# A two-layer Mamba and attention kernel: the scan's B and C rows in one PSUM bank, the freed bank for projections, outputs and turned rows

## The chip, the cores and the metric

One core of one Trainium2 chip runs the whole program in one launch. The metric is the device time of a launch in microseconds (us). A core has five engines that each work through their own queue in order: TensorE (PE), VectorE (DVE), ScalarE (ACT), GpSimd (POOL) and SyncE (SP, which here only starts DMAs). They wait for each other by semaphores. PE writes into PSUM, 8 banks of 128 partitions x 512 float32; DVE and ACT read it.

## The reference

The input is 8 sequences of 512 tokens with 128 features. Two residual layers follow each other.

```
x = x + mamba_and_filter(layernorm(x)) + mixture_of_2_experts(layernorm(x))     # layer 0
x = x + attention(layernorm(x)) + routed_experts(layernorm(x))                  # layer 1

# the scan of layer 0, for each of 256 inner features and 16 states n:
h[t] = exp(delta[t] * A[n]) * h[t-1] + delta[t] * B[t, n] * u[t]
y[t] += h[t] * C[t, n]

# the attention of layer 1, 16 heads of 64, causal, q and k rotated (rope):
attn = softmax(q k^T / 8);  out = (attn v) wo^T + bo

# routed experts: each token goes to its best 2 of 8 experts, silu(x W1) * (x W3) W2
```

## The kernel before

The 8 sequences are pipelined. Each pass of the loop ("lap") has two phases for sequence b. Phase 1 runs the rest of layer 0 for b (`filter_step`), the routed experts of b-1 (`token_use`), the start of layer 0 for f = b+1 (`front_start`) and that sequence's first two scan states (`early_scan`). Phase 2 runs the attention of b together with the other 14 scan states of f, gathers the expert rows of b-1 and scatters the token rows of b. Every engine's order is written out by hand in its own `phase_1` and `phase_2`. Lap 0 has no b-1, lap 7 no f.

The attention has 8 pairs of heads. A pair takes 4 steps (t_ = 0 to 3, one per 128 query tokens), so phase 2 has 32 steps s. A step handles two score tiles, n = 2s and 2s+1 (one per head), of width (t_+1) x 128. For a tile the work goes around three engines: PE makes the scores (`scores`, L1006 and L1009), DVE takes the row maximum (`largest`, L1803), ACT the exponential (`exponentials`, L1304), PE transposes the result (`turn`, L1017), ACT copies it out of PSUM (`copy_turned`, L1312), PE multiplies with the values (`weigh_values`, L1032). Scores of step s+2 are made in step s. At t_ = 0 DVE divides the pair before by its sums (`divide`, L1815).

The queries and keys of the pair after next are projected in steps t_ = 2 and 3 (`project`, L994). Projection m passes DVE (`rotate`, L1797, which multiplies by the sine into ROT3), SP (`swap_pairs`, a DMA from ROT3), ACT (`add_bias`, L1288) and POOL (`add_rotated`, L1936 and L1939). In steps t_ = 1 PE transposes the finished output of the pair before (`turn_out`, L1041) and ACT copies it (`copy_out`, L1322). Step 12 transposes the gathered rows (`give_back`, L929), steps 24, 26, 27 and 28 the routed rows (`turn_rows`, L890).

A scan state n has three parts on DVE (`front_step`): part 0 (D, L1504) multiplies DU with B row n, part 1 (the scan, L1509) needs exponentials from ACT (DA, L1191), part 2 (H, L1531) multiplies with C row n into HC, which POOL adds to Y (L1925). B and C rows are spread over the partitions by a matmul each (`front_b`, L767, into bank FB; `front_c`, L774, into bank FC). The table `PIECES` says in which step each part stands.

Banks in phase 2: FB and FC for the scan, G2 for turned tiles, G3 for attention sums, and a ring of four (G1, G0, FM, G4) for scores. Projections, outputs and turned rows have no bank of their own: the table `loan` lends them ring bank `RING[2*s % 4]` between score tile 2s and score tile 2s+4. A borrower therefore waits until the exponential of tile 2s has been read (`(p_exp, 2*s_+1)`), and score tile 2s+4 waits until the borrower has been read. PE issues the projection of step s already in step s-1, before `weigh_values`. DVE's `rotate` stands first in step s, ahead of `largest`; ACT's `add_bias` or `copy_out` stands second in step s, behind the first `copy_turned`.

DVE has one more wait in phase 2: `number_places` in step 9 (L1784) waits until POOL has added the gathered rows of b-1 (`add_picks`, L1955, at tile 17).

Of the kernel before, what the change touches and what calls it, by code (L numbers as in the profile page):

```python
# [35 lines left out]
P = 128  # L36
# [87 lines left out]
def build(nc, xT, weights, vecs, conv_rows, dt_w, a_log, moe, experts,  # L124
          row_biases, cos, sin, identity, causal, row_of, in_u_w, outT):
    ctx = ExitStack()
    with ctx:
# [348 lines left out]
        loan = {}  # L476
        for s_ in range(STEPS):
            j_, t_ = s_ // TILES, s_ % TILES
            if s_ < 2:
                loan[s_] = (("proj", 2 + s_), (biased, 3 + s_))  # L480
            if t_ in PROJECT_AT and j_ + 2 < PAIRS:
                m_ = 2 * (j_ + 2) + PROJECT_AT.index(t_)
                loan[s_] = (("proj", m_), (biased, m_ + 1))
            if t_ == OUT_STEP and j_:
                loan[s_] = (("out", j_ - 1), (ot_copy, j_))
            if s_ == RETURN_STEP:
                loan[s_] = (("return", 0), (out_d, 0))
            if s_ in TURN_STEPS and s_ not in loan:
                g_ = TURN_STEPS.index(s_)
                loan[s_] = (("turn", g_), (xt_copy, g_ + 1))  # L490
# [10 lines left out]
        ring_bank["out", PAIRS - 1], ring_free["out", PAIRS - 1] = RING[0], [(p_exp, N_TILES - 3)]  # L501
        assert len(set(k for k, _ in loan.values())) == len(loan)
# [164 lines left out]
        def _(pe):  # L667
# [88 lines left out]
            def front_b(b, n, filtered=None, bank=FB):  # L756
# [8 lines left out]
                if filtered is not None and n == EARLY:  # L765
                    pe.wait_ge(xn2_d.sem, xn2_d.at(filtered))
                pe.matmul(bank[:, :], pick[:, n, :], S3[:, :], start=True, stop=True).then_inc(b_mm.sem, 1)  # L767

            def front_c(b, n, filtered=None):
# [4 lines left out]
                pe.matmul(FC[:, :], pick[:, STATES + n, :], S3[:, :], start=True, stop=True).then_inc(c_mm.sem, 1)  # L774

# [294 lines left out]
            def phase_2(b, f, t):  # L1070
# [4 lines left out]
                if f is not None:  # L1075
                    front_b(f, EARLY, b)
                    front_c(f, EARLY, b)
                values_in(b, f)
                rows_out(b)
                rank(b)  # L1080
# [6 lines left out]
                project(b, 2)  # L1087
                for s in range(STEPS):
                    j, t_ = s // TILES, s % TILES
                    key = loan[s][0] if s in loan else (None, None)  # L1090
                    following = loan[s + 1][0] if s + 1 in loan else (None, None)
                    if key[0] == "out":
# [7 lines left out]
                    turn(b, 2 * s)  # L1100
                    if s:
                        weigh_values(b, 2 * s - 1)
                    if f is not None:
                        for n, part in PIECES[s]:
                            if part == 0:
                                front_b(f, n, b)
                            elif part == 1:
                                front_c(f, n, b)
                    turn(b, 2 * s + 1)
# [32 lines left out]
        def _(act):  # L1142
# [190 lines left out]
            def phase_2(b, f, t):  # L1333
# [10 lines left out]
                for s in range(STEPS):  # L1344
                    copy_turned(b, 2 * s)
                    key = loan[s][0] if s in loan else (None, None)
                    if key[0] == "proj":
                        add_bias(b, key[1])
                    elif key[0] == "out":
                        copy_out(b, key[1])  # L1350
                    elif key[0] == "turn":
                        rows_turned(b, key[1])
# [11 lines left out]
                    if s + 1 < STEPS:  # L1364
                        exponentials(b, 2 * s + 3, f)
                copy_out(b, PAIRS - 1)
# [11 lines left out]
        def _(dve):  # L1378
# [119 lines left out]
            def front_step(b, n, part, early=False):  # L1498
# [602 lines left out]
```

## Time and profile before

| | |
|---|---|
| three runs | 2735.15 us median, 2718.67 to 2745.57 |
| the profiled execution | 2738.27 us, of which the span 2736.5 |
| PE busy | 2185.6 us, 80% of the span |
| DVE busy | 1644.7 us, 60% |
| ACT busy | 1177.2 us, 43% |
| POOL busy | 936.8 us, 34% |
| mean granted PE clock | 0.869 of full |
| chain that ended last | PE 49%, issue 17%, DVE 15%, POOL 9%, ACT 7% |

Busy is the time in which an engine has an instruction of its own in work. The granted clock is the share of 2.4 GHz that PE was given; it has two levels, 1.2 and 2.4 GHz, so 0.50 in a stretch is the lower one throughout. A wait is named by who waited and whose instruction released it.

### The profile page before, as it was taken

How to read it: one execution, taken by the hardware profiler on the slowest of the kernel's cores; microseconds unless marked ns; L12 is line 12 of the kernel's file. 1: busy time of each engine (PE TensorE's matmuls, PEld its weight loads, DVE VectorE, ACT ScalarE, POOL GpSimd, SP SyncE). 2: the span in 40 equal slices, each digit the busy share in tenths (PEclk: the TensorE clock that was granted, in tenths of full speed). 3: DMA queues.
4: the chain of work that ended last, by engine and by line, in shares of the span. 5: the costliest groups of instructions: out<-in, count | busy, mean ns of one | idle time of the engine just before them, and what ended most of it. 6: DMA issues, size and time to landing. Idle time of an engine off the chain costs nothing.

```text
span 2736.5 us, 38788 instructions
## 1 busy us (share of the span) xinstructions
PE 2185.6 (80%) x11640; PEld 1519.0 (56%) x11640; DVE 1644.7 (60%) x2929; ACT 1177.2 (43%) x2702; POOL 936.8 (34%) x581
## 2 busy tenths in 40 slices
PE   4257888888888788888889788987889788888885
PEld 1033566655665556655566556655666555665664
DVE  2965775557754776547764587546765477644322
ACT  2223454345533455345543465333553345423541
POOL 0421562028410473006620185103740067202501
PEclk8568889888999889989899898898899988999997
DMA  2000011311222111321113112221113211131123
GB/s 94 0 16 0 32 50 62 113 51 46 68 82 75 53 41 58 106 76 41 51 64 104 61 46 70 70 88 50 44 59 97 85 37 56 59 126 58 62 93 115
DMA packets 82452, 175.06 MB, mean 64 GB/s; under 512 B 11448, under 2 KB 42560, under 8 KB 81984
## 3 DMA queue, kind: packets, MB, share of 16 engines
q1 hardware_dynamic: 78144, 164.05, 17.9%
q0 software_dynamic: 4096, 8.40, 1.1%
q8 instruction: 107, 1.75, 0.3%
q14 instruction: 105, 0.86, 0.1%
HBM read 123.71 MB, written 15.14 MB: 51 GB/s over the span
## 4 chain that ended last, share of the span: by engine, by line
PE 49%; issue 17%; DVE 15%; POOL 9%; ACT 7%; DMA 1%; SPq 0%; DVEq 0%; POOLq 0%; ACTq 0%
PE G L910 8%; PE G L1032 6%; DVE HS L1509 3%; PE G L1017 3%; POOL Y L1925 3%; PE G L921 2%; PE FM L1006 2%; POOL REG L1936 2%; PE G L1049 2%; PE FM L731 2%; POOL YG L1950 2%; DVE maxes L1803 2%; PE G L1006 2%; POOL REG L1939 2%; PE FM L880 2%
## 5 line engine op out<-in xcount | busy, mean ns | idle before, releaser
L1032 PEld LDWEIGHTS G<-REG 128*128 128x128 f32 x2560 | 376.8, 213 | 79.2 <-issue 53.6
L1032 PE MATMUL G<-REG 128*128 128x64 f32 x2560 | 383.7, 286 | 18.9 <-DVE REG L1815 18.9
L1312 ACT ACTIVATE REG<-G 128x128 f32<-128x128 f32 (+3 forms) x512 | 224.1, 438 | 374.9 <-PE G L1017 371.5
L1509 DVE TENSOR_TENSOR_SCAN HS<-DA,D 128x1024 f32<-128x1024 f32 x128 | 361.8, 2827 | 31.3 <-ACT DA L1191 30.7
L1925 POOL TENSOR_TENSOR Y<-Y,HC 128x1024 f32<-128x1024 f32 x114 | 274.8, 2410 | 258.0 <-DVE HC L1531 257.4
L910 PEld LDWEIGHTS G<-XGT,MW 128*128 128x128 f32 x1920 | 294.9, 238 | 58.1 <-issue 58.1
L910 PE MATMUL G<-XGT,MW 128*128 128x128 f32 x1920 | 301.9, 324 | 19.5 <-DMA MW<-moe 19.5
L1936 POOL TENSOR_TENSOR REG<-REG,cos_t 128x512 f32<-128x512 f32 x128 | 170.4, 1331 | 341.8 <-ACT REG L1288 340.7
L1017 PE MATMUL G<-ident,REG 128*128 128x128 f32 x1280 | 248.1, 295 | 31.0 <-ACT REG L1312 29.4
L1006 PE MATMUL G<-REG 64*128 64x128 f32 (+3 forms) x768 | 233.4, 517 | 12.1 <-ACT REG L1288 6.1
L1261 ACT ACTIVATE SL<-G 128x512 f32<-128x512 f32 x120 | 71.6, 597 | 375.9 <-PE G L910 375.9
L1676 DVE SCALAR_TENSOR_TENSOR SL<-SL,G 128x512 f32<-128x512 f32 x120 | 82.5, 688 | 237.1 <-ACT SL L1261 237.1
L1939 POOL TENSOR_TENSOR REG<-REG 128x512 f32<-128x512 f32 x128 | 200.6, 1567 | 48.5 <-DMA REG<-ROT 36.8
L1191 ACT ACTIVATE DA<-DELTA,a_neg 128x511 f32<-128x511 f32 x256 | 180.8, 721 | 63.2 <-DVE HS L1509 62.9
L1304 ACT ACTIVATE REG<-G,maxes 128x128 f32<-128x128 f32 (+3 forms) x384 | 196.9, 513 | 18.1 <-DVE maxes L1803 18.1
L1017 PEld LDWEIGHTS G<-ident,REG 128*128 128x128 f32 x1280 | 158.7, 154 | 78.1 <-issue 70.8
L1803 DVE TENSOR_REDUCE maxes<-G 128x1 f32<-128x128 f32 (+3 forms) x384 | 165.7, 459 | 27.1 <-PE G L1009 27.0
L1504 DVE TENSOR_TENSOR D<-DU,FB 128x1024 f32<-128x1024 f32 x114 | 138.4, 1214 | 40.4 <-PE FB L767 37.8
L1903 POOL TENSOR_SCALAR Y<-US,V_ 128x512 f32<-128x512 f32 x16 | 24.8, 1559 | 387.7 <-ACT US L1165 353.8
L1909 POOL TENSOR_TENSOR DU<-DELTA,US 128x1024 f32<-128x1024 f32 x8 | 18.8, 2350 | 388.6 <-DVE DELTA L1496 388.6
L921 PE MATMUL G<-MW,HC 128*128 128x128 f32 x960 | 142.7, 297 | 9.9 <-DVE HC L1683 9.9
L921 PEld LDWEIGHTS G<-MW,HC 128*128 128x128 f32 x960 | 133.8, 215 | 11.5 <-DVE HC L1683 8.0
(284 smaller groups left out, 3972.0 us busy)
## 6 DMA issues: line engine op xcount, KB each, us to landing
MW<-moe SPq DMA_DIRECT2D x120, 768.0 KB, 4.3
REG<-ROT SPq DMA_DIRECT2D x256, 128.0 KB
EW<-experts SPq DMA_DIRECT2D x16, 514.5 KB, 4.2
XG<-x_rows SPq DMA_DIRECT2D x8, 960.0 KB, 5.6
y_rows<-YO SPq DMA_DIRECT2D x120, 64.0 KB, 1.5
X<-xT SPq DMA_DIRECT2D x8, 256.0 KB, 5.7
W<-weights SPq DMA_DIRECT2D x1, 2048.0 KB, 9.4
REG<-xT SPq DMA_DIRECT2D x8, 256.0 KB, 2.8
```

What stands on the lines that cost most here:

```text
L910: mm = pe.matmul(G[g + half][:, c * P:(c + 1) * P], MW[:, i % SLOTS, at:at + P], XGT[:, i, :], start=True, stop=True)
L921: mm = pe.matmul(G[4][:, 0:D], HH[:, i % 4, c * P:(c + 1) * P], MW[:, i % SLOTS, 2 * HID + c * D:2 * HID + (c + 1) * D], start=c == 0, sto ...
L1006: pe.matmul(bank[:, 0:width], QK[lo:lo + DK, j % 2, 0, t * P:(t + 1) * P], QK[lo:lo + DK, j % 2, 1, 0:width], start=True, stop=False)
L1017: mm = pe.transpose(G[2][:, c * P:(c + 1) * P], PR[:, n % 2, c * P:(c + 1) * P], ident[:, :])
L1032: mm = pe.matmul(G[3][:, col:col + DK], PT[:, n % 2, c * P:(c + 1) * P], V[:, c, j * P + h * DK:j * P + (h + 1) * DK], start=c == 0, stop= ...
L1304: act.activation(PR[:, n % 2, 0:width], ring_bank[("score", n)][:, 0:width], ACT.Exp, bias=maxes[:, j % 2, at:at + 1], accum_out=rows[:, j ...
L1312: act.activation(PT[:, n % 2, 0:width], G[2][:, 0:width], ACT.Copy).then_inc(pt_copy.sem, 1)
L1509: dve.tensor_tensor_scan(HS[:, :, :].rearrange("p h s -> p (h s)"), DA[:, n % 2, :, :].rearrange("p h s -> p (h s)"), D1[:, :, :].rearrang ...
L1803: dve.tensor_reduce(maxes[:, j % 2, at:at + 1], ring_bank[("score", n)][:, 0:width], AX.X, ALU.max, negate=True).then_inc(nm_d.sem, 1)
L1925: pool.tensor_tensor(Y[:, :, :], Y[:, :, :], HC_EARLY if early else HC[:, n % 2, :, :], ALU.add).then_inc(y_add.sem, 1)
L1936: pool.tensor_tensor(rotated, rotated, cos_t[:, :], ALU.mult).then_inc(rope_d.sem, 1)
L1939: pool.tensor_tensor(rotated, rotated, REG[:, 8 + m % 2, :], ALU.add).then_inc(rope_d.sem, 1)
```

## The change

The scan's B and C rows of states 2 to 15 take turns in FB. A new `main_b` waits until H of the state before has read its C row, a new `main_c` until D of its own state has read the B row. FC becomes `MISC`, the bank of all projections, outputs and turned rows of phase 2 (`guest` in place of `loan`); each guest waits for the guest before it to be read, and scores wait for exponentials only. The guest's PE work moves behind `turn(b, 2*s+1)` of its own step s, `rotate` and `give_back` move to the end of DVE's step, `add_bias`, `copy_out` and `rows_turned` to the end of ACT's step. Part 2 of a state is placed by an offset of 1.45 in place of 1.7, which brings H of states 4, 6, 8 and 15 one step forward. The front loop of lap 0 and the early scan keep their banks.

```diff
@@ tables
-                PIECES[int(at_ + (0.0, 0.7, 1.7)[part_])].append((n_, part_))
+                PIECES[int(at_ + (0.0, 0.7, 1.45)[part_])].append((n_, part_))
+        PICKS_AT = {s_: [] for s_ in range(STEPS)}
+        for n_ in range(FIRST, STATES):
+            d_ = next(s_ for s_ in PIECES if (n_, 0) in PIECES[s_])
+            h_ = next(s_ for s_ in PIECES if (n_, 2) in PIECES[s_])
+            PICKS_AT[d_].append((n_, 0))
+            PICKS_AT[max(d_ + 1, h_ - 1)].append((n_, 1))
...
-            if n_ >= 4 and n_ % 2 == 0 and n_ // 2 - 2 in loan:
-                ring_free["score", n_] = [loan[n_ // 2 - 2][1]]
-        for s_, (key, freed) in loan.items():
-            ring_bank[key], ring_free[key] = RING[2 * s_ % 4], [(p_exp, 2 * s_ + 1)]
+        freed_ = []
+        for s_, (key, freed) in guest.items():
+            ring_bank[key], ring_free[key], freed_ = MISC, freed_, [freed]
@@ PE
+            def main_b(b, n, filtered):
+                if n == EARLY:
+                    pe.wait_ge(xn2_d.sem, xn2_d.at(filtered))
+                pe.wait_ge(hc_mul.sem, hc_mul.at(b, n))
+                pe.matmul(FB[:, :], pick[:, n, :], S3[:, :], start=True, stop=True).then_inc(b_mm.sem, 1)
+            def main_c(b, n):
+                pe.wait_ge(db_mul.sem, db_mul.at(b, n + 1))
+                pe.matmul(FB[:, :], pick[:, STATES + n, :], S3[:, :], start=True, stop=True).then_inc(c_mm.sem, 1)
@@ PE, phase_2
-                project(b, 2)
                 for s in range(STEPS):
...
+                    turn(b, 2 * s)
+                    if s:
+                        weigh_values(b, 2 * s - 1)
+                    if f is not None:
+                        for n, part in PICKS_AT[s]:
...
+                    turn(b, 2 * s + 1)
+                    if key[0] == "proj":
+                        project(b, key[1])
+                    elif key[0] == "out":
                         turn_out(b, key[1])
...
-                    if following[0] == "proj":
-                        project(b, following[1])
@@ ACT, phase_2
                     copy_turned(b, 2 * s)
-                    if key[0] == "proj":
-                        add_bias(b, key[1])
...
                         exponentials(b, 2 * s + 3, f)
+                    if key[0] == "proj":
+                        add_bias(b, key[1])
@@ DVE, phase_2
-                    if key[0] == "proj":
-                        rotate(b, key[1])
                     if s + 1 < STEPS:
                         largest(b, 2 * s + 2)
                         largest(b, 2 * s + 3)
...
                         for n, part in PIECES[s]:
                             front_step(f, n, part)
+                    if key[0] == "proj":
+                        rotate(b, key[1])
```

The instruction order shows three places. In it `HS<-DA,D` is the scan, `ROT<-` is `rotate`, `maxes<-` is `largest`, and `HC<-` and `D<-` are H and D of a state.

DVE before, lap 0, from H of state 2 (ahead of step 0) to the start of step 1:

```order
L1531 TENSOR_TENSOR HC<-HS,FC 128x1024
L1797 SCALAR_TENSOR_TENSOR ROT<-G,V_,sin_t 128x512
L1803 TENSOR_REDUCE maxes<-FM 128x1
L1803 TENSOR_REDUCE maxes<-G 128x1
L1504 TENSOR_TENSOR D<-DU,FB 128x1024
L1509 SCALAR_TENSOR_TENSOR HS<-DA,D 128x1024
L1797 SCALAR_TENSOR_TENSOR ROT<-FM,V_,sin_t 128x512
```

DVE after, the same place:

```order
L1549 TENSOR_TENSOR HC<-HS,FB 128x1024
L1821 TENSOR_REDUCE maxes<-FM 128x1
L1821 TENSOR_REDUCE maxes<-G 128x1
L1522 TENSOR_TENSOR D<-DU,FB 128x1024
L1527 SCALAR_TENSOR_TENSOR HS<-DA,D 128x1024
L1815 SCALAR_TENSOR_TENSOR ROT<-FC,V_,sin_t 128x512
```

The first `rotate` (projection 2) moved from ahead of D and the scan of state 3 to behind them, and reads FC.

ACT before, lap 0, steps 0 and 1 (L1312 `copy_turned`, L1288 `add_bias`, L1304 exponentials, L1191 DA):

```order
L1312 ACTIVATE REG<-G 128x128
L1288 ACTIVATE REG<-G,V_ 128x512
L1304 ACTIVATE REG,rows<-FM,maxes 128x256
L1191 ACTIVATE DA<-DELTA,a_neg 128x511
L1312 ACTIVATE REG<-G 128x128
L1191 ACTIVATE DA<-DELTA,a_neg 128x511
L1304 ACTIVATE REG,rows<-G,maxes 128x256
L1312 ACTIVATE REG<-G 128x256
```

ACT after, the same place (L1330 `copy_turned`, L1306 `add_bias`, L1322 exponentials, L1209 DA):

```order
L1330 ACTIVATE REG<-G 128x128
L1322 ACTIVATE REG,rows<-FM,maxes 128x256
L1209 ACTIVATE DA<-DELTA,a_neg 128x511
L1330 ACTIVATE REG<-G 128x128
L1209 ACTIVATE DA<-DELTA,a_neg 128x511
L1322 ACTIVATE REG,rows<-G,maxes 128x256
L1306 ACTIVATE REG<-FC,V_ 128x512
L1330 ACTIVATE REG<-G 128x256
```

`add_bias` moved from behind the first copy of its step to directly ahead of the first copy of the next step.

PE before, lap 0, steps 0 and 1 (L994 projection, L1017 `turn`, L767 and L774 B and C row, L1006 and L1009 scores, L1032 `weigh_values`):

```order
L994 MATMUL G<-XN,W 128x512
L1017 MATMUL G<-ident,REG 128x128
L767 MATMUL FB<-S,pick 128x512
L774 MATMUL FC<-S,pick 128x512
L1017 MATMUL G<-ident,REG 128x128
L1006 MATMUL G<-REG 128x384 x2
L1009 MATMUL G<-causal_bf,ident_bf 128x128 x2
L994 MATMUL FM<-XN,W 128x512
L1032 MATMUL G<-REG 128x64
L1017 MATMUL G<-ident,REG 128x128 x2
```

PE after, the same place (L1010 projection, L1033 `turn`, L786 and L790 B and C row, L1022 and L1025 scores, L1048 `weigh_values`):

```order
L1033 MATMUL G<-ident,REG 128x128
L786 MATMUL FB<-S,pick 128x512
L1033 MATMUL G<-ident,REG 128x128
L1010 MATMUL FC<-XN,W 128x512
L1022 MATMUL G<-REG 128x384 x2
L1025 MATMUL G<-causal_bf,ident_bf 128x128 x2
L1048 MATMUL G<-REG 128x64
L1033 MATMUL G<-ident,REG 128x128 x2
L1048 MATMUL G<-REG 128x64
L790 MATMUL FB<-S,pick 128x512
```

Both projections stand one turn later, and the C row of state 3 moved from beside its B row into step 1.

## Rows read from the trace of the kernel before

**Rows 1.** The page: shares of the chain that ended last, by engine.

```profile
PE 49%; issue 17%; DVE 15%; POOL 9%; ACT 7%; DMA 1%; SPq 0%; DVEq 0%; POOLq 0%; ACTq 0%
```

**Rows 2.** Windows, phase 2 of laps 2 and 7: stretch, length, busy by engine, PEclk, DMA.

```profile
924.00:1094.00 170.00, 144.84 (x833) 98.82 (x831) 121.45 (x172) 96.51 (x259) 107.85 (x66) 0.89 0.15 51
...
2504.00:2634.00 130.00, 112.86 (x772) 80.44 (x771) 54.41 (x128) 79.20 (x228) 58.38 (x50) 1.00 0.18 61
```

**Rows 3.** Waits over the whole span: total us, times, longest us.

```profile
PE FM L994 <- ACT REG L1304: 54.9, 48, 4.2
PE G L994 <- ACT REG L1304: 54.7, 48, 2.7
...
PE G L1017 <- ACT REG L1312: 29.4, 116, 0.5
...
DVE place_i L1784 <- POOL YG L1955: 24.9, 7, 5.1
```

**Rows 4.** Windows inside phase 2 of lap 2.

```profile
936.00:985.00 49.00, 38.73 (x238) 24.88 (x234) 38.07 (x55) 30.04 (x84) 43.53 (x27) 0.96 0.13 44
985.00:1005.00 20.00, 17.80 (x74) 13.51 (x75) 12.26 (x19) 7.57 (x21) 16.05 (x11) 0.50 0.16 57
1005.00:1032.00 27.00, 20.50 (x129) 13.22 (x128) 23.53 (x23) 16.61 (x45) 15.90 (x10) 1.00 0.23 74
1032.00:1046.00 14.00, 14.00 (x65) 11.04 (x64) 6.69 (x11) 5.22 (x16) 6.12 (x4) 0.51 0.06 20
```

**Rows 5.** Timelines of DVE, ACT, PE around 1028 us: start, us, engine, line, idle before.

```profile
1025.50 3.46 DVE L1509 TENSOR_TENSOR_SCAN HS<-DA,D 128x1024 f32<-128x1024 f32 x1 [1.11 <-ACT DA L1191]
1028.89 0.72 DVE L1797 SCALAR_TENSOR_TENSOR ROT<-G,V_,sin_t 128x512 f32<-128x512 f32 x1
...
1029.64 0.69 ACT L1288 ACTIVATE REG<-G,V_ 128x512 f32<-128x512 f32 x1 [1.96 <-DVE ROT L1797]
1030.24 0.69 ACT L1304 ACTIVATE REG<-FM,maxes 128x512 f32<-128x512 f32 x1
...
1031.07 1.13 PE L994 MATMUL FM<-XN,W 128*128 128x512 f32 x2 [2.72 <-ACT REG L1304]
```

**Rows 6.** Timelines of POOL, DVE, PE around 984 us.

```profile
982.39 1.26 POOL L1955 TENSOR_TENSOR YG<-YG 128x512 f32<-128x512 f32 x1
...
983.85 0.17 DVE L1784 CAST place_i<-places 128x8 uint32<-128x8 f32 x1 [5.12 <-POOL YG L1955]
...
985.25 0.61 PE L774 MATMUL FC<-S,pick 96*128 96x512 bf16 x1 [2.72 <-DVE HC L1531]
...
988.45 2.08 PE L994 MATMUL FM<-XN,W 128*128 128x512 f32 x2 [1.95 <-ACT REG L1304]
```

**Rows 7.** Timelines of DVE, ACT, POOL in steps 0 and 1 of lap 2.

```profile
937.80 0.75 DVE L1797 SCALAR_TENSOR_TENSOR ROT<-G,V_,sin_t 128x512 f32<-128x512 f32 x1 [0.46 <-PE G L994]
...
941.15 2.29 DVE L1509 TENSOR_TENSOR_SCAN HS<-DA,D 128x1024 f32<-128x1024 f32 x1 [0.80 <-ACT DA L1191]
...
938.59 0.69 ACT L1288 ACTIVATE REG<-G,V_ 128x512 f32<-128x512 f32 x1 [0.40 <-DVE ROT L1797]
...
941.81 0.38 ACT L1312 ACTIVATE REG<-G 128x256 f32<-128x256 f32 x1 [0.23 <-PE G L1017]
...
939.73 1.27 POOL L1936 TENSOR_TENSOR REG<-REG,cos_t 128x512 f32<-128x512 f32 x1
...
945.72 1.28 POOL L1936 TENSOR_TENSOR REG<-REG,cos_t 128x512 f32<-128x512 f32 x1
```

**Rows 8.** PE timeline: eight value matmuls at the full and at the half clock.

```profile
1037.34 1.81 PE L1032 MATMUL G<-REG 128*128 128x64 f32 x8
...
1071.28 1.00 PE L1032 MATMUL G<-REG 128*128 128x64 f32 x8
```

**Rows 9.** Waits in lap 7's phase 2.

```profile
PE G L994 <- ACT REG L1304: 4.4, 7, 0.8
PE FM L994 <- ACT REG L1304: 3.9, 6, 0.7
```

More of the change, by code:

```diff
@@ L479, in build @@
             if s_ < 2:
-                loan[s_] = (("proj", 2 + s_), (biased, 3 + s_))
+                guest[s_] = (("proj", 2 + s_), (biased, 3 + s_))
             if t_ in PROJECT_AT and j_ + 2 < PAIRS:
                 m_ = 2 * (j_ + 2) + PROJECT_AT.index(t_)
-                loan[s_] = (("proj", m_), (biased, m_ + 1))
+                guest[s_] = (("proj", m_), (biased, m_ + 1))
             if t_ == OUT_STEP and j_:
-                loan[s_] = (("out", j_ - 1), (ot_copy, j_))
+                guest[s_] = (("out", j_ - 1), (ot_copy, j_))
             if s_ == RETURN_STEP:
-                loan[s_] = (("return", 0), (out_d, 0))
-            if s_ in TURN_STEPS and s_ not in loan:
+                guest[s_] = (("return", 0), (out_d, 0))
+            if s_ in TURN_STEPS and s_ not in guest:
                 g_ = TURN_STEPS.index(s_)
-                loan[s_] = (("turn", g_), (xt_copy, g_ + 1))
+                guest[s_] = (("turn", g_), (xt_copy, g_ + 1))
         ring_bank, ring_free = {}, {}
@@ L1086, in phase_2 @@
                 scores(b, 1)
-                project(b, 2)
                 for s in range(STEPS):
                     j, t_ = s // TILES, s % TILES
-                    key = loan[s][0] if s in loan else (None, None)
-                    following = loan[s + 1][0] if s + 1 in loan else (None, None)
-                    if key[0] == "out":
+                    key = guest[s][0] if s in guest else (None, None)
+                    turn(b, 2 * s)
+                    if s:
+                        weigh_values(b, 2 * s - 1)
+                    if f is not None:
+                        for n, part in PICKS_AT[s]:
+                            if part == 0:
+                                main_b(f, n, b)
+                            else:
+                                main_c(f, n)
+                    turn(b, 2 * s + 1)
+                    if s == 0 and f is not None:
+                        pe.wait_ge(hc_mul.sem, hc_mul.at(f, EARLY))
+                    if key[0] == "proj":
+                        project(b, key[1])
+                    elif key[0] == "out":
                         turn_out(b, key[1])
@@ L1099, in phase_2 @@
                             give_back(t, returned)
[L1100 to L1109, printed above, removed]
                     if t_ == 0 and s + 2 < STEPS:
                         scores(b, s + 2)
-                    if following[0] == "proj":
-                        project(b, following[1])
                     weigh_values(b, 2 * s)
@@ L1345, in phase_2 @@
                     copy_turned(b, 2 * s)
-                    key = loan[s][0] if s in loan else (None, None)
-                    if key[0] == "proj":
-                        add_bias(b, key[1])
[L1349 to L1352, printed above, removed]
+                    key = guest[s][0] if s in guest else (None, None)
                     if s + 1 < STEPS:
@@ L1365, in phase_2 @@
                         exponentials(b, 2 * s + 3, f)
+                    if key[0] == "proj":
+                        add_bias(b, key[1])
+                    elif key[0] == "out":
+                        copy_out(b, key[1])
+                    elif key[0] == "turn":
+                        rows_turned(b, key[1])
                 copy_out(b, PAIRS - 1)
@@ L1496, in softplus_end, with front_step @@
                 dve.tensor_tensor(DELTA[:, :, :], HS[:, :, :], DELTA[:, :, :], ALU.add).then_inc(delta_d.sem, 1)
-            def front_step(b, n, part, early=False):
+            def front_step(b, n, part, b_bank=FB, c_bank=FB, early=False):
                 if part == 0:
@@ L1852, in phase_2 @@
                         largest(b, 2 * s + 3)
-                    if key[0] == "return" and t is not None:
-                        give_back(t, ring_bank[key])
                     if t_ == 0 and j:
@@ L1865, in phase_2 @@
                             front_step(f, n, part)
+                    if key[0] == "proj":
+                        rotate(b, key[1])
+                    elif key[0] == "return" and t is not None:
+                        give_back(t, ring_bank[key])
                 divide(b, PAIRS - 1)
@@ L1872, in front @@
                     for part in range(3):
-                        front_step(b, n, part)
+                        front_step(b, n, part, FB, FC)
             def late():
@@ L1992, in phase_2 @@
                     s = n // 2
-                    key = loan[s][0] if n % 2 == 0 and s in loan else (None, None)
+                    key = guest[s][0] if n % 2 == 0 and s in guest else (None, None)
                     if t is not None and n in GATHER_AT:
```

21 lines of the change are left out of this document (10 added, 11 removed).

## The prediction

> **What bounds the kernel now.** I read the page's chain first: PE carries 49% of it, DVE 15%, POOL 9% [rows 1]. No engine is full, so the question is where phase 2 hands over. The windows show that phase 2 takes 170 us in lap 2, with PE busy for 144.84, DVE for 121.45 and POOL for 107.85 [rows 2]. Lap 7, which has no scan, takes 130 us for the same attention at the full clock [rows 2]. So 40 us of a lap's phase 2 is the price of running the scan beside it, and the stages inside show how it arises [rows 4]:
>
> - 936 to 985 us: POOL is busy for 43.53 of 49. DVE then stands 5.12 us at `number_places` until POOL's last add of gathered rows is done [rows 6]. POOL sets the end of this stage; no PE or DVE wait saved before 984 is worth anything in laps 1 to 6. Over the span DVE loses 24.9 us at that wait in 7 laps [rows 3].
> - 985 to 1005: granted clock 0.50 (1.2 GHz), PE busy for 17.80 of 20. PE had stood still for 2.72 us and, just after, for 1.95 [rows 6].
> - 1005 to 1032: clock 1.00, DVE busy for 23.53 of 27, PE for 20.50. Here DVE sets the pace.
> - 1032 to 1046: clock 0.51, PE busy for all 14.00, DVE for 6.69. PE sets the pace because it is slow. It had stood for 2.72 us at a projection just before [rows 5].
>
> The projection's wait is the borrowed bank: L994 waits for the exponential L1304 96 times, 54.9 and 54.7 us, together 109.6 us [rows 3], which is 4.0% of the span and the ceiling of the direct gain.
>
> **The change, part by part.**
>
> *No instruction is added or removed.* The same B, C, projection and transpose matmuls run; only banks, waits and places differ. Work is priced at nothing; the waits are the sum.
>
> *Projections no longer wait for the exponential.* What the 109.6 us are worth depends on the stage. Before 984 us: nothing (POOL). The wait of 1.95 us at 988.45 lies in the half-clock stage, where PE has nothing else to do: worth 1.95. The 2.72 us wait at 1031.07 is a chain of a slow scan (3.46 us), `rotate`, `add_bias`, exponential, projection [rows 5]. After the change, `rotate` still stands behind a scan on DVE, and ACT's next `copy_turned` stands behind `add_bias`, so PE's second `turn` of the next step waits for the same chain. But PE has its projection, value matmuls and next scores to issue first, and the stall breaks into two of 1 to 1.5 us. I take 1.2 us saved of the 2.72.
>
> *The half-clock lapse after it.* It is priced from rows at either level: eight value matmuls take 1.81 us at the half clock and 1.00 at the full [rows 8], so the 14.00 us of PE work from 1032 to 1046 shrinks to 14.00 x 1.00/1.81 = 7.7. With PE busy throughout that saves 6.3; at the busy share of the full-clock stage, 20.50/27 = 0.76, it takes 10.1 and saves 3.9 [rows 4]. I take 5. The single long stall is the only thing that separates 1032 from the 27 us ahead of it, which held 1.00 with PE idle a quarter of the time in pieces. So I expect this lapse to go, in laps 0 to 6. Together: 6.2 us per lap.
>
> *`rotate` behind D and the scan.* In step 0 of lap 2 `rotate` ran at 937.80, `add_bias` at 938.59, and POOL took the result at 939.73, the moment it was free [rows 7]. Now the scan stands ahead. It started at 941.15 after 0.80 of waiting for DA and took 2.29; with `add_bias` out of ACT's way I put its end at 942.6, `rotate` to 943.35, `add_bias` to 944.1, POOL at 944.2: 4.5 us late, on the engine that sets this stage. POOL has 49 - 43.53 = 5.5 us idle in it, which can swallow some. Bounds 0 and 4.5, taken 3.0 per lap in laps 1 to 6. DVE's 5.12 us wait grows by as much.
>
> *ACT held.* ACT's copy at 941.81 [rows 7] now stands behind that `add_bias` and runs near 944.1. Queued behind it are the exponentials of the step; PE waits with its second `turn`, for some 3 us, in each of the first steps. In laps 1 to 6 POOL covers it; in lap 0 it costs something, taken 1 us.
>
> *B and C in one bank.* B row n+1 waits until H of state n is read; in `PIECES` H always ends an earlier step than the next D, so DVE has at least two row maxima in between, under which the matmul of the B row fits. C row n waits for D of its own state and is used a step later. Cover: those maxima. Without the cover each of 13 states costs at most the 0.61 us that such a matmul took at the half clock [rows 6], 8 us a lap. Taken 0.
>
> *Lap 7* has no scan, so `rotate` and `add_bias` follow the projection at once; PE waits 4.4 + 3.9 = 8.3 us there [rows 9], and I take 6 of it.
>
> *Sum.* Middle laps: +3.0 - 1.95 - 6.2 = -5.15, six times -30.9. Lap 0: -6.2 + 1 = -5.2. Lap 7: -6. Together -42 us. The profiled execution took 2738.3 us, 3.1 more than the median of the three runs; 2735.15 - 42 = 2693, given as 2694.
>
> **A rule against it.** The full-clock stage shows that a PE idle for a quarter of the time in short waits (109.6/96 = 1.14 us on average at the projections) keeps 1.00 [rows 3, 4]. The Trainium skill, "TensorE: Matmul & The Clock Gate", section "A second HAM failure mode: psum-queue depth-cycling", says that a kernel cycling through PSUM banks can micro-idle between groups often enough for the clock to oscillate. By that page the many short waits that I expect would be no safer than the one long one, and the sum would keep its lapses. No row here shows it for waits this short.
>
> **Rivals.**
>
> *A. The stalls move and the lapse stays* (0.27). The chain scan, `rotate`, `add_bias`, copy, `turn` is as long as the old one, so PE still stands long enough once a lap. For it: DVE is the pace at the full clock, 23.53 of 27, and its work is unchanged. Against: PE has more to issue ahead of the wait. Then middle laps give +3.0 - 1.95 = +1.05, lap 0 +1, lap 7 -6: 2735 + 6.3 + 1 - 6 = 2736.
>
> *B. ACT behind DVE makes it slower* (0.21). Place: the end of steps t_ = 2 and 3, where ACT now may not copy the next tile until DVE has done D, scan, H and `rotate`. It decides if the stall of PE there exceeds the 2.72 us of before, which takes two slow scans (3.46 in place of 2.29) close together, or D, a slow scan and H in one stretch. Then a further lapse per lap comes on: 6.3 + 2.7 = 9 us in 7 laps, 63, beside A's +1: 2736 + 63 = 2799; with a lapse in half the laps, 2768. The first steps, with ACT held for 3 us each, are where it would begin. For it: DVE was first in line before and is last now. Against: in the first stage POOL covers it.
>
> *C. PE gains everywhere after 984* (0.17). Laps 0 to 6 hold (109.6 - 8.3)/7 = 14.5 us of projection waits each, of which 1.95 and 2.72 are priced above; of the 9.8 left about a third stand behind 984 us, so 3 us more are gained, the lapse is worth 6.3 + 2.72, and POOL absorbs its delay: -(1.95 + 9.0 + 3) = -14 in 6 laps, -12 in lap 0, -8.3: 2735 - 104 = 2631; halfway to it, 2662.
>
> **How the numbers follow.** The forecast, lapse gone and POOL 3 us later, has 0.35, and its own range is 2670 to 2715. A differs from no change by less than 1%, about what a measurement of this kernel can tell from none. The ends: below, C's halfway point and somewhat more, 2650, from POOL's bound of 0 (-18 us) and the lapse at 6.3; above, B with a lapse in most laps, 2785. That leaves about 1 in 10 on each side. Faster by over 1% (below 2708) is C and most of the forecast: 0.17 + 0.31 = 0.48. Within 1%: A, the rest of the forecast and a little of B, 0.27 + 0.04 - 0.01 = 0.30. Slower by over 1%: B, and 0.01 of A, 0.22.
>
> **What the profile after would show.** Right: the L994 waits on L1304 gone; phase 2 of laps 0 to 6 with one long stretch at 0.50 in place of two, clock near 0.9 or above in phase 2; a wait of some 8 us at `number_places`; the first POOL multiply of step 0 some 4 us later after the first scores; PE's new waits at the second `turn` behind `copy_turned`, none over 2 us past step 10. Wrong: waits of PE on ACT's copy or on H that sum to more than 15 us a lap; three or more half-clock stretches in a lap; DVE waiting for B rows; or POOL's last gather add not later at all.

## The result and the profile after

The changed kernel takes 2752.95 us (median of 20 runs), the kernel before, on the same chip, 2732.92 us (20 runs): a ratio of 1.0073, interval 1.0049 to 1.0097. The forecast of 2694 us, faster, was wrong. The time lies inside its range of 2650 to 2785, but 59 us above the forecast, between rival A (2736) and the lower end of rival B (2768); a change of under 1% had a chance of 0.30. The profiled execution of the changed kernel has a span of 2746.1 us, that of before 2736.5.

The wait that the change was to take away is gone. In the page's costliest groups (busy us, mean ns, then idle time before it) the projection stands with nothing ahead of it, where it had 109.6 us [rows 3]:

```profile
L1010 PE MATMUL FC<-XN,W 128*128 128x512 f32 x224 | 142.8, 725 | 0.0
```

The waits over the whole span (total us, times, longest us) show what came in its place. The line numbers have moved: L1033 is `turn`, L1330 `copy_turned`, L1306 `add_bias`, L1815 `rotate`, L786 and L790 the B and the C pick, L1973 POOL's last add of gathered rows.

```profile
ACT REG L1306 <- DVE ROT L1815: 153.1, 107, 10.7
...
PE G L1033 <- ACT REG L1330: 109.4, 126, 3.2
...
PE FB L786 <- DVE HC L1549: 40.8, 28, 4.1
...
DVE place_i L1802 <- POOL YG L1973: 33.7, 7, 4.9
PE FB L790 <- DVE D L1522: 33.2, 12, 4.0
```

PE waited 29.4 us for ACT's copy before [rows 3], now 109.4: waits of 80 us came up at that one line for the 109.6 us that went, and 74 us at the two picks with them. Phase 2 of lap 2 as a whole (columns as in [rows 2]) has a granted clock of 0.85 where it had 0.89:

```profile
924.00:1094.00 170.00, 142.78 (x818) 99.24 (x817) 125.92 (x172) 98.60 (x258) 102.70 (x66) 0.85 0.15 50
...
936.00:992.00 56.00, 45.39 (x236) 29.76 (x232) 40.38 (x54) 30.88 (x84) 40.76 (x27) 0.79 0.12 39
...
958.00:973.00 15.00, 15.00 (x67) 10.38 (x67) 9.52 (x12) 7.00 (x21) 13.75 (x9) 0.58 0.13 43
992.00:1005.00 13.00, 9.24 (x35) 6.99 (x36) 8.90 (x9) 4.45 (x12) 7.14 (x6) 0.61 0.07 25
1032.00:1046.00 14.00, 11.15 (x63) 8.06 (x62) 9.98 (x14) 7.78 (x21) 7.20 (x6) 0.76 0.35 109
1058.00:1072.00 14.00, 13.59 (x62) 9.55 (x62) 7.13 (x10) 7.79 (x23) 7.15 (x5) 0.63 0.49 170
```

The stretch 1032 to 1046 has come up from 0.51 [rows 4] to 0.76, but 958 to 973 and 1058 to 1072 are new ones, and the first stage, which stood at 0.96, is at 0.79. Read from edge to edge, the granted clock is 0.50 in six stretches of this phase 2: 943.2 to 949.9, 956.9 to 970.4, 987.6 to 990.9, 994.4 to 1004.5, 1035.4 to 1042.1 and 1059.3 to 1069.4, 50 us in all. Before there were three, 37 us: 947.0 to 950.3, 984.6 to 1004.9 and 1032.3 to 1045.9. So the stretch behind 1032 isn't gone, it has become shorter and begins during a wait of 2.85 us at PE's `turn`. The timelines show what led to it (a slow scan, the row maxima behind it, the exponential, ACT's copy), and how the last of the six begins (scan, `rotate`, `add_bias`, copy, `turn`):

```profile
1029.46 5.19 DVE L1527 TENSOR_TENSOR_SCAN HS<-DA,D 128x1024 f32<-128x1024 f32 x1 [0.64 <-ACT DA L1209]
...
1035.27 0.69 ACT L1322 ACTIVATE REG<-FM,maxes 128x512 f32<-128x512 f32 x1 [4.32 <-DVE maxes L1821]
...
1036.57 1.09 PE L1033 MATMUL G<-ident,REG 128*128 128x128 f32 x4 [2.85 <-ACT REG L1330]
...
1054.03 2.29 DVE L1527 TENSOR_TENSOR_SCAN HS<-DA,D 128x1024 f32<-128x1024 f32 x1 [0.88 <-ACT DA L1209]
...
1056.23 0.73 DVE L1815 SCALAR_TENSOR_TENSOR ROT<-FC,V_,sin_t 128x512 f32<-128x512 f32 x1
...
1056.99 0.69 ACT L1306 ACTIVATE REG<-FC,V_ 128x512 f32<-128x512 f32 x1 [2.33 <-DVE ROT L1815]
...
1057.58 0.59 ACT L1330 ACTIVATE REG<-G 128x512 f32<-128x512 f32 x1
...
1058.31 0.63 PE L1033 MATMUL G<-ident,REG 128*128 128x128 f32 x4 [2.53 <-ACT REG L1330]
```

At the end of the second chain PE stands 2.53 us, and the eight value matmuls that follow at 1060.06 take 1.80 us, the half-clock price of [rows 8]. And POOL, which sets the first stage, runs dry three times. Its timeline of the first multiply of `rope` (L1954) in lap 2:

```profile
943.42 1.27 POOL L1954 TENSOR_TENSOR REG<-REG,cos_t 128x512 f32<-128x512 f32 x1 [3.63 <-ACT REG L1306]
...
957.33 2.85 POOL L1954 TENSOR_TENSOR REG<-REG,cos_t 128x512 f32<-128x512 f32 x1 [2.50 <-ACT REG L1306]
...
976.48 1.27 POOL L1954 TENSOR_TENSOR REG<-REG,cos_t 128x512 f32<-128x512 f32 x1 [3.16 <-ACT REG L1306]
...
991.00 1.26 POOL L1973 TENSOR_TENSOR YG<-YG 128x512 f32<-128x512 f32 x1
```

The last add stood at 982.39 [rows 6] and is at 991.00, although this lap's first `turn` is 1.0 us earlier (936.64 for 937.60). The idle times, 3.63 + 2.50 + 3.16 = 9.3 us, are all waits for `add_bias`. DVE, too, comes to `number_places` 8.9 us later, at 987.60 for 978.73, and then waits about as long as before [rows 6]; PE's C pick behind it stands 4.03 us:

```profile
992.46 2.13 DVE L1802 CAST place_i<-places 128x8 uint32<-128x8 f32 x1 [4.86 <-POOL YG L1973]
...
995.76 0.61 PE L790 MATMUL FB<-S,pick 96*128 96x512 bf16 x1 [4.03 <-DVE D L1522]
```

### The profile page after: what moved, and what is told of

Its sections match the earlier page's. It is cut to its first block, busy times and chain, and to the rows that moved or that the text cites. A ratio compares the mean times of both kernels' runs of the same rounds, so it can differ in the third digit from the quotient of the medians.

```text
span 2746.1 us, 38800 instructions
## 1 busy us (share of the span) xinstructions
PE 2175.3 (79%) x11640; PEld 1518.3 (55%) x11640; DVE 1657.5 (60%) x2929; ACT 1195.3 (44%) x2702; POOL 920.4 (34%) x581
## 4 chain that ended last, share of the span: by engine, by line
PE 48%; issue 16%; DVE 15%; POOL 11%; ACT 6%; DMA 2%; SPq 1%; DVEq 0%; POOLq 0%; ACTq 0%
PE G L926 8%; PE G L1048 6%; PE G L1033 4%; DVE HS L1527 4%; POOL Y L1943 3%; POOL REG L1954 3%; POOL YG L1968 2%; PE FC L1010 2%; PE G L937 2%; PE FM L1022 2%; PE G L1065 2%; PE FM L738 2%; POOL REG L1957 2%; PE FM L896 2%; ACT REG L1330 2%
## 5 line engine op out<-in xcount | busy, mean ns | idle before, releaser
L1048 PEld LDWEIGHTS G<-REG 128*128 128x128 f32 x2560 | 386.0, 217 | 71.4 <-issue 51.2
L1048 PE MATMUL G<-REG 128*128 128x64 f32 x2560 | 390.2, 290 | 3.1 <-DVE REG L1833 3.1
L1527 DVE TENSOR_TENSOR_SCAN HS<-DA,D 128x1024 f32<-128x1024 f32 x128 | 351.0, 2742 | 19.3 <-ACT DA L1209 18.7
L1033 PE MATMUL G<-ident,REG 128*128 128x128 f32 x1280 | 260.7, 307 | 110.7 <-ACT REG L1330 109.4
L1954 POOL TENSOR_TENSOR REG<-REG,cos_t 128x512 f32<-128x512 f32 x128 | 183.0, 1430 | 378.7 <-ACT REG L1306 378.0
L1330 ACT ACTIVATE REG<-G 128x128 f32<-128x128 f32 (+3 forms) x512 | 222.9, 435 | 198.6 <-PE G L1033 194.8
L1033 PEld LDWEIGHTS G<-ident,REG 128*128 128x128 f32 x1280 | 162.8, 161 | 155.2 <-issue 125.0
L1022 PE MATMUL G<-REG 64*128 64x128 f32 (+3 forms) x768 | 237.5, 523 | 7.4 <-POOL REG L1957 6.4
L1322 ACT ACTIVATE REG<-G,maxes 128x128 f32<-128x128 f32 (+3 forms) x384 | 194.7, 507 | 58.0 <-DVE maxes L1821 58.0
L1209 ACT ACTIVATE DA<-DELTA,a_neg 128x511 f32<-128x511 f32 x256 | 179.9, 717 | 63.2 <-DVE HS L1527 62.9
L1957 POOL TENSOR_TENSOR REG<-REG 128x512 f32<-128x512 f32 x128 | 178.3, 1393 | 67.5 <-DMA REG<-ROT 61.9
L1010 PE MATMUL FC<-XN,W 128*128 128x512 f32 x224 | 142.8, 725 | 0.0
L937 PE MATMUL G<-MW,HC 128*128 128x128 f32 x960 | 132.6, 283 | 11.1 <-DVE HC L1701 11.1
```

The source lines that it names most:

```text
L937: mm = pe.matmul(G[4][:, 0:D], HH[:, i % 4, c * P:(c + 1) * P], MW[:, i % SLOTS, 2 * HID + c * D:2 * HID + (c + 1) * D], start=c == 0, sto ...
L1010: pe.matmul(bank[:, :], w(name, j * P), XN2[:, :], start=True, stop=True).then_inc(pj_mm.sem, 1)
L1022: pe.matmul(bank[:, 0:width], QK[lo:lo + DK, j % 2, 0, t * P:(t + 1) * P], QK[lo:lo + DK, j % 2, 1, 0:width], start=True, stop=False)
L1033: mm = pe.transpose(G[2][:, c * P:(c + 1) * P], PR[:, n % 2, c * P:(c + 1) * P], ident[:, :])
L1048: mm = pe.matmul(G[3][:, col:col + DK], PT[:, n % 2, c * P:(c + 1) * P], V[:, c, j * P + h * DK:j * P + (h + 1) * DK], start=c == 0, stop= ...
L1322: act.activation(PR[:, n % 2, 0:width], ring_bank[("score", n)][:, 0:width], ACT.Exp, bias=maxes[:, j % 2, at:at + 1], accum_out=rows[:, j ...
```

## The experiments

Three theories. **T1**: the new places cost: `rotate` behind D and the scan, `add_bias` at the end of ACT's step, the projection in its own step; the banks are a gain. **T2**: one bank for B and C costs, since PE now waits for D and H. **T3**: nothing is gained or lost, half-clock stretches only move about. Thirteen kernels were run; all ratios are to the kernel before, measured beside them.

**The banks alone.** New banks, H at 1.45, every guest at its old place.

```
 # PE                               # DVE, ACT
 scores(b, 0); scores(b, 1)          rotate(b, key[1])      # ahead of largest
+project(b, 2)   # ahead of loop     largest, largest, D, scan, H
 for s: guest; turn(2s); ...         copy_turned(b, 2 * s)
   scores; project(following)        add_bias / copy_out    # behind first copy
```

> The changed banks alone: B and C rows take turns in one bank, the guests (projection, output, turned rows) have the other, but every guest stands where it stood before: projection one step ahead, rotate first in DVE's step, add_bias and copy_out behind ACT's first copy. Theory T1 (the slowdown comes from the places: rotate and add_bias at the end of the step hold ACT's copy, PE's turn waits for it): the banks cost nothing, PE's waits for ACT's copy_turned fall from 109 us back to some 30, projections wait for no exponential, POOL's last gathered add in lap 2 comes back from 54 to about 45 us after the first turn; 2650 to 2720 us, ratio to the kernel before 0.97 to 0.995. Theory T2 (one bank for B and C makes PE wait for DVE's H and D): 2745 to 2770 us, ratio 1.005 to 1.015, as slow as the changed kernel. Theory T3 (half-clock stretches only move about): ratio 1.00 within 0.5%.

Measured: 2671.69 us, ratio 0.9761 (0.9721 to 0.9801). T2 by itself is out as the cause: the sharing of the bank is in this kernel and it is 2.4% faster. T3 is out as well, which had this kernel within 0.5% of the one before. Whether the sharing costs something together with the new places was not tested; the waits at the two picks sum to 50 us here and to 74 in the changed kernel. Against the changed kernel the places are worth 1.0073/0.9761 = 3.2%, some 85 us. The waits show why:

```profile
PE FC L1010 <- ACT REG L1308: 45.8, 25, 3.9
...
PE G L1033 <- ACT REG L1332: 36.0, 124, 2.2
...
PE FB L790 <- DVE D L1524: 25.8, 7, 5.2
```

The `turn` waits are down from 109.4 to 36.0; a projection waits 45.8 us for the `add_bias` of the guest before it, since there is one guest bank.

**The places alone.** Old banks and loans, new places.

```
-project(b, 2) ahead of the loop; project(following) in step s - 1
+turn(b, 2 * s + 1); guest (proj, out, turn, return)      # PE
-rotate first, add_bias behind first copy
+rotate last, add_bias last
```

> The changed places alone: guests borrow score banks as before, B and C keep a bank each, but projections follow the second turn of their own step, rotate and give_back stand last in DVE's step, add_bias and copy_out last in ACT's. T1: slower than the kernel before, at least as slow as the changed one, since the scores behind a guest now wait for an add_bias that comes a step's length later: 2760 to 2860 us, ratio 1.01 to 1.045. T2: the places are harmless, ratio 0.995 to 1.005. T3: ratio 1.00 to 1.02.

Measured: 2947.39 us, 1.0762 (1.073 to 1.0794). The direction is T1's; the loss of 7.6% is 1.7 times its upper bound of 4.5%. The reason that the expectation gave is seen: with a borrowed score bank the scores behind a guest wait for an `add_bias` that stands at ACT's end.

```profile
PE G L1006 <- ACT REG L1286: 140.0, 56, 4.9
```

With the same wait in the other score banks (42.2 us) these are 182 us. So the new places are far worse without the free bank, and this kernel doesn't tell what they cost beside it.

**B and C in one bank, and H's place.** Three kernels make a square with the kernel before.

```
-front_b -> FB, front_c -> FC           # a bank each
+main_b, main_c -> FB, PICKS_AT          # one bank, loans kept
-(0.0, 0.7, 1.7)[part_]
+(0.0, 0.7, 1.45)[part_]
```

The sharing with H at 1.7:

> The kernel before with one edit: the main scan's B and C rows take turns in one bank (H's place kept at 1.7), the other bank stands empty, loans and places as before. T1: nothing gained and nothing lost, ratio 0.996 to 1.006, PE's waits for DVE's H and D at the picks under 3 us a lap. T2: slower, ratio 1.007 to 1.015, with those waits the growth. T3: ratio 1.00 within 1%, with the half-clock stretches at other places than before.

The sharing with H at 1.45:

> The kernel before with B and C in one bank, and H at 1.45: the sharing as the change has it, loans and places as before. If the 0.4% that the same with H at 1.7 cost came from H's place: ratio 0.996 to 1.001. If it is the sharing itself: 1.003 to 1.007.

H at 1.45 without sharing:

> The kernel before with one edit: H's place at 1.45 in place of 1.7 steps behind D; B and C keep a bank each. With the two sharing kernels it makes a square of four: sharing alone (H at 1.7) was 1.0039, sharing with H at 1.45 1.0002. If sharing costs nothing once H is early: this one 0.998 to 1.002. If H's earlier place is a gain of its own, which the sharing takes back: 0.990 to 0.997.

Measured: 1.0039 (1.0018 to 1.0061); 1.0002 (0.9971 to 1.0033); 0.9987 (0.9971 to 1.0002). With H late the sharing costs 0.4%, with H early nothing that can be measured. The expectation that the first has under 3 us of waits a lap was wrong:

```profile
PE FB L787 <- DVE HC L1549: 70.8, 21, 6.9
```

At 1.7, H(n) falls into the step of D(n+1) for three of the 13 states, 4, 6 and 8 (with 32 steps for 13 states, state 4 has H at int(2.46 + 1.7) = 4, and state 5 its D at int(4.92) = 4). Over 7 laps these are the 21 waits of the line. PE's B pick, ahead of the second `turn`, waits for all of it. At 1.45 that total is 16.5 us. With free guests the same edit on the banks-alone kernel:

> The banks-alone kernel with H's place back at 1.7 steps behind D, as in the kernel before. There H(n) stands in the same step as D(n+1) for about half of the states, so the B pick on PE waits for it ahead of the second turn. T1: those waits for H and D grow from 50 us to 90 us over the span and PE's turns with them: ratio to the kernel before 0.978 to 0.988. If H's place is nothing: 0.974 to 0.978.

Measured 0.9833 (0.9774 to 0.9892), 86.9 us of waits for H at the B pick (24.1 us with H at 1.45). The size fits, and the count is 21 again (the expectation's "about half of the states" was too many), but the interval overlaps that of the banks-alone kernel, so this is likely, not shown.

**`rotate` moved up.** The changed kernel, one edit.

```
 largest(b, 2 * s + 2); largest(b, 2 * s + 3)
+rotate(b, key[1])
 front_step(f, n, part)    # D, scan, H
-rotate(b, key[1])
```

> The changed kernel with one edit: DVE's rotate stands directly behind the step's two row maxima, ahead of D, scan and H. Projection, add_bias and all banks as changed. T1: in the first two steps POOL gets its rows some 3 to 5 us earlier, PE's waits for ACT's copy fall from 109 us to 50 to 80, POOL's last add of lap 2 comes near 50 us after the first turn; 2700 to 2735 us, ratio to the kernel before 0.985 to 1.0. T2: no effect, ratio 1.005 to 1.01. T3: within 0.5% of the kernel before, whichever waits go.

Measured 2698.99 us, 0.9861 (0.9835 to 0.9886): moving `rotate` up recovers 2.1 of the 3.2%. But not by the way expected: POOL's last add in lap 2 came 52.1 us after the first `turn`, hardly earlier than the changed kernel's 54.4. The waits say that DVE now stands for PE:

```profile
DVE ROT L1815 <- PE FC L1010: 155.7, 87, 3.2
...
PE G L1033 <- ACT REG L1330: 67.7, 119, 2.9
```

**ACT's guest a step later.** The changed kernel, one edit.

```
 copy_turned(b, 2 * s)
+add_bias / copy_out / rows_turned of guest[s - 1]
 ...
-add_bias / copy_out / rows_turned of guest[s]     # at the end
```

> The changed kernel with one edit: ACT's add_bias, copy_out and rows_turned of a step stand in the next step behind its first copy_turned, so that this copy no longer stands behind an add_bias that waits for rotate. Theory H (holding ACT's copy, and PE's second turn with it, is what costs): PE's waits for ACT's copy fall from 109 us to 30 to 60, ratio to the kernel before 0.985 to 1.0. Rival O (the place of rotate, and POOL's late start with it, is what costs; add_bias only comes later still): 1.0 to 1.015.

Measured 2717.73 us, 0.9918 (0.9887 to 0.9948): theory H. PE's waits for the copy are 31.9 us in place of 109.4. Letting the copy go first is worth 1.6% although `add_bias` itself comes later.

**The first two projections back.** The changed kernel, with tiles 2 and 3 at their old places on PE, DVE and ACT.

```
+project(b, 2)                       # ahead of the loop
 for s: ... if s == 0: project(b, 3) # rotate first, add_bias behind first copy, s < 2
```

> The changed kernel with the projections of steps 0 and 1 alone (tiles 2 and 3) put back to their old places on PE, DVE and ACT; all later guests as changed. Theory P (the cost sits in the first two steps, where POOL sets the end and its last gathered add came 8.6 us later in lap 2): 6 to 8 us a lap come back, ratio to the kernel before 0.983 to 0.993, POOL's last add in lap 2 some 45 us after the first turn. Rival Q (the cost is spread over all guests, in the pairs behind the gather): ratio 0.998 to 1.006.

Measured 2724.38 us, 0.9969 (0.9936 to 1.0002): 1.0% below the changed kernel, between the two theories; P's mechanism is there (POOL's last add at 49.3 us in lap 2, 48.0 on average), at half its price. With `rotate` moved up as well:

> The changed kernel with both edits that brought something back: the projections of steps 0 and 1 at their old places, and rotate of all later ones directly behind the two row maxima. If the two effects (2.1% and 1.0% below the changed kernel) are separate: ratio to the kernel before 0.973 to 0.981, as the banks-alone kernel. If both cured the same delay of POOL in the first steps: 0.983 to 0.990.

Measured 2697.87 us, 0.9864 (0.9834 to 0.9895), no better than `rotate` alone: the two don't add up. The ratio is the one that the expectation gave for a common delay of POOL in the first steps, but that reason isn't borne out: POOL's last add comes at 49.4 us here and at 52.9 with `rotate` alone, and the time is the same.

**Both places, PE's kept.** `rotate` up and ACT's guest a step later together; the projection stays in its own step.

> The changed kernel with two edits together: rotate directly behind the two row maxima, and ACT's add_bias, copy_out and rows_turned in the next step behind its first copy_turned. Every projection stays behind the second turn of its own step. Theory R (rotate's place and ACT's place are the whole cost, PE's place of the projection is harmless): ratio to the kernel before 0.970 to 0.980, as the banks-alone kernel, PE's waits for ACT's copy under 45 us. Rival S (the missing 1% lies in the place of the projection on PE): 0.983 to 0.990, no better than rotate alone.

Measured 2704.46 us, 0.9885 (0.9846 to 0.9924): rival S. PE's waits for the copy are down to 35.2 us, as in the banks-alone kernel, and 1.3% is still missing. The waits point at the projection's own place: issued behind the second `turn` of the step in which `rotate` wants it, DVE waits for it, with D and the scan queued behind:

```profile
DVE ROT L1815 <- PE FC L1010: 117.6, 79, 3.3
```

In the banks-alone kernel, where it is issued a step ahead, that wait is 19.5 us. This is argued from the waits and not shown by one edit. The two kernels also differ in `rotate`, which stands behind the maxima here and ahead of them there, in ACT's guest, a step later here, and in the place of outputs and turned rows on PE; and the waits at the two picks are 117 us here (62.0 and 55.4), 50 there.

**ACT's guest last, everything else old.** The banks-alone kernel with the ACT place of the changed one.

> The banks-alone kernel (guests at their old places) with one edit: ACT's add_bias, copy_out and rows_turned stand last in ACT's step as in the changed kernel; projections and rotate stay at their old places. Theory T1a (what costs is that add_bias waits for a rotate behind D and the scan; ACT's own place is harmless if rotate is done early): ratio to the kernel before 0.974 to 0.984, close to the banks-alone kernel. Rival T1b (add_bias behind both exponentials makes POOL late by itself in the first steps): 0.985 to 0.998.

Measured 3080.76 us, 1.1279 (1.1215 to 1.1342), far off both theories. A projection a step ahead must wait until the one guest bank is read, and ACT reads it at the end of the step before:

```profile
PE FC L1010 <- ACT REG L1308: 143.4, 64, 2.9
...
PE FC L1010 <- ACT EW L1342: 70.0, 32, 3.2
```

PE waits there ahead of the very value matmuls and scores on which ACT's exponentials depend. So the places come as a set: guests a step ahead on PE need ACT's copy at the front of its step. The opposite mixture, `rotate` last and `add_bias` first, would wait on itself (the scan needs DA, DA stands behind `add_bias` on ACT, `add_bias` needs `rotate`). That is read from the order of the queues; it wasn't run.

**The projection later within its step.** The banks-alone kernel, one edit.

```
 turn(b, 2 * s + 1); scores (t_ == 0)
-project(b, following[1])
 weigh_values(b, 2 * s); scores (t_ > 0)
+project(b, following[1])
```

> The banks-alone kernel with one edit: the projection that is issued a step ahead stands behind the value matmuls and scores of its step, ahead of nothing but the next step, so that add_bias of the guest before has longer. In the banks-alone kernel PE waits 45.8 us in 25 places for that add_bias. T1: these waits fall under 20 us, POOL's last gathered add unchanged at 45 to 47 us after the first turn; ratio to the kernel before 0.965 to 0.976. Rival: the projection comes too late for rotate at the top of the next step, where the two row maxima stand behind it, and DVE waits instead: 0.976 to 0.99.

Measured 2664.09 us, 0.973 (0.9701 to 0.976): the fastest kernel here, with the banks-alone kernel's interval overlapping. Both sides of the expectation are seen: PE's wait for `add_bias` fell from 45.8 to 14.0 us, DVE's for the projection rose from 19.5 to 57.4.

**Where in a lap it lies.** From PE's and POOL's timelines of each profiled execution, means over laps 1 to 6, us: from the first `turn` to the start of POOL's last gathered add; from there to the first `project_out`; from there to the next lap's first `turn` (gaps behind laps 0 to 5).

| kernel | to POOL's last add | to the outputs | rest of lap | sum |
|---|---|---|---|---|
| before | 45.3 | 103.3 | 173.3 | 321.9 |
| sharing, H at 1.45, loans kept | 44.8 | 103.7 | 173.5 | 322.0 |
| banks alone | 45.5 | 96.0 | 171.5 | 313.0 |
| changed | 53.7 | 101.9 | 169.2 | 324.8 |
| changed, ACT's guest later | 48.7 | 99.5 | 171.9 | 320.1 |
| changed, first two back | 48.0 | 99.2 | 172.1 | 319.3 |
| changed, `rotate` up | 52.9 | 94.4 | 169.6 | 316.9 |
| changed, `rotate` up and first two back | 49.4 | 95.5 | 171.5 | 316.4 |
| changed, both places | 51.3 | 94.9 | 171.9 | 318.1 |
| banks alone, projection later | 45.7 | 95.5 | 170.6 | 311.8 |

The free bank is worth 103.7 - 96.0 = 7.7 us a lap behind the gather and nothing ahead of it. The new places cost 53.7 - 45.5 = 8.2 ahead of it and 101.9 - 96.0 = 5.9 behind it. `rotate` up brings 7.5 us behind the gather and 0.8 ahead of it. ACT's guest later and the first two projections back bring 5.0 and 5.7 ahead of it, and 2.4 and 2.7 behind it. These parts overlap, so they can't be added.

## Why the prediction was wrong, step by step

- *What the free bank gives* was right in its sum, in part by luck. The sum had 1.95 + 1.2 + 5 in six laps, 6.2 in lap 0 and 6 in lap 7, together 61 us. The pair that differs in the loans and the guests' bank alone, 1.0002 and 0.9761, gives 2.4%, 66 us. Of its parts, the stage behind the gather gave 7.7 us a lap for 8.15. Lap 0 gave 1.2 for 6.2 (134.7 to 133.5 us from the first `turn` to the first `project_out`, one lap of one execution each), and 2.0 us a lap came in phase 1, some 12 in all, where the sum had nothing. Lap 7 went from 120.6 to 113.8 us between first `turn` and first `project_out`: 6.8 for the 6 taken.
- *Where the forecast was lost.* Phase 2 of laps 1 to 6 was to become 5.15 us a lap shorter and became 7.0 longer. Two terms of the sum failed: POOL's delay (8.4 us for 3.0) and the gain behind the gather (1.4 us for 8.15), over six laps 32 and 40 us.
- *POOL late by 3.0 us a lap* came out as 8.4 (45.3 to 53.7), well past its bound of 4.5. The delay of the first projection was worked out right: POOL's first multiply came 6.8 us after the first `turn` for 2.1 before, 4.7 later for the 4.5 of the sum. The step stopped there. Every further projection that POOL takes in this stage stands behind the same chain. So POOL, which had not waited for ACT between its first multiply and its last add, waited three times, 9.3 us. Its idle time could swallow nothing: the long piece of it, 2.47 us, lies ahead of the Y add at 937.42, where it still is (2.44), and the rest was in pieces of 0.31 us and less.
- *"In laps 1 to 6 POOL covers it"* failed as reasoning. PE's 3 us wait in the first step came as forecast (3.10 us at 943.76), but the engine that was to cover it waits for the same `add_bias`. The wait at `number_places` was to grow to some 8 us and is 4.86, since DVE itself is 8.9 us late: the whole circle of engines was slowed, and not POOL alone. Letting ACT's copy go first brought POOL's add back from 53.7 to 48.7 and the time by 1.6%.
- *The lapse behind step 18* was to go, and stayed: it is shorter (0.76 in its stretch for 0.51), and a second one stands 24 us behind it. The argument was that the single long stall alone separates it from a stretch at 1.00, and that PE's new waits would be 1 to 1.5 us, "none over 2 us past step 10". There were one of 2.85 at 1036.57 and one of 2.53 at 1058.31. The failed step is that the stall would break into two short ones. At 1058.31 the chain scan, `rotate`, `add_bias`, copy still ended at PE, even behind a scan of 2.29 us and not the slow one of 3.46 [rows 5]. At 1036.57 the prediction had the wrong path: a scan of 5.19 us reached PE through the row maxima, the exponential and the copy, and neither `rotate` nor `add_bias` is in it. The stage behind the gather gained 1.4 us (103.3 to 101.9) for the 8.15 summed.
- *Rival B* had the mechanism and the place: ACT behind DVE at the end of t_ = 2 and in the first steps. Its numbers, 2768 to 2799, are above the measured 2753. They had no gain in phase 1, which gave back 25 us (see below). It asked for slow scans; the wait at 1036.57 had one, the wait at 1058.31 came without. The text named, among what would show it wrong, waits on ACT's copy and on H of over 15 us a lap: 109.4 + 40.8 over 8 laps is 19.
- *B and C in one bank at nothing*: right, since the change moved H to 1.45 with it; at 1.7 it costs 0.4%. Measured is that with the guests at their old places; in the changed kernel the picks wait 74 us, with one wait of 4.03 us at the start of a stretch at 0.50 (994.4).
- *Phase 1* is in no term of the sum, put at nothing without a word. It became 4.1 us a lap shorter (173.3 to 169.2), 25 us over six gaps. About 1 to 2 us of each is the projection of tile 2 that moved into the loop (1.02 us at the full clock, 1.92 at the half); why the rest came is open. Without it the change would have been slower by more.
- *The rule weighed.* The lapses stayed in the sum, as the Trainium skill, "TensorE: Matmul & The Clock Gate", section "A second HAM failure mode: psum-queue depth-cycling", would have had it. But in phase 2 of lap 2 of the changed kernel the stretches at half clock stand at waits of 2.5 to 4.0 us, or of 1.71 and 1.57 us 2 us apart, not at short ones as the rule describes, so that trace doesn't bear it out. Nor does the length of the wait alone settle it: in the kernel before, the waits of 2.67, 2.72 and 2.72 us at 945.42, 985.25 and 1031.07 go with stretches of 3.3, 20.3 (with a further wait of 1.95 us in it) and 13.6 us at 0.50.

## What to carry to other kernels

A guest operation that passes through several engines in order has one place in each queue, and the places are a set: moving one to the end of its step lets everything queued behind it on the next engine wait for the step's longest operation. Before counting on an engine as cover for another's wait, follow whether it waits for the same producer, and for each item of the stage, not the first alone. Where a change frees a resource and moves work as well, cost and try the two apart: here one was 2.4% faster and the other took 3.2% back.

## What the runs showed of the hardware

In the banks-alone kernel the same phase-1 instructions take one of two lengths (169 or 174 us), from lap to lap of one execution. Windows, from the first `project_out` of laps 0 and 1 to the first `turn` of the next:

```profile
432.69:602.03 169.34, 140.92 (x699) 98.23 (x698) 90.27 (x223) 59.59 (x99) 21.08 (x12) 0.91 0.24 78
741.74:915.65 173.91, 146.55 (x698) 103.19 (x698) 90.20 (x223) 59.59 (x99) 21.03 (x12) 0.88 0.23 76
557.69:592.69 35.00, 23.34 (x137) 19.56 (x136) 23.34 (x45) 10.51 (x19) 6.00 (x3) 0.85 0.19 62
866.74:901.74 35.00, 24.91 (x127) 22.16 (x127) 21.68 (x42) 8.59 (x15) 4.72 (x2) 0.71 0.16 53
432.69:557.69 125.00, 108.99 (x523) 74.44 (x523) 58.87 (x152) 42.98 (x67) 9.28 (x6) 0.92 0.26 86
741.74:866.74 125.00, 108.50 (x516) 74.15 (x516) 58.28 (x151) 42.17 (x65) 9.21 (x6) 0.92 0.26 86
```

The first 125 us agree to 0.5 us of PE work at clock 0.92; the 35 us behind them run at 0.85 in one lap and at 0.71 in the other, and the lap is 4.6 us longer. In the kernel before the gaps are 172.0 to 174.0 us, in the changed one 168.1 to 171.4: part of what the changed kernel lost in phase 2 it got back here, in code that the change doesn't touch. What decides between the two lengths stays open; no run varied it alone. Single laps of one profile are therefore good to no better than 5 us, and a gain of a few us a lap in one phase has to be read off whole laps.
